# Outputs of the second layer's short row tiles transposed by DMA, their projection three slots later, expert weight pieces in the long row tiles

## What is computed

```python
q = (xn @ Wq).reshape(b, n, H, DH).transpose(0, 2, 1, 3) * scale
sim = jnp.einsum('bhid,bjd->bhij', q, k) + bias
sim = jnp.where(causal_mask, neg, sim)
sim = jnp.where(mask_p[:, None, None, :], sim, neg)
attn = jax.nn.softmax(sim, axis=-1)
out = jnp.einsum('bhij,bjd->bhid', attn, v)
out = out.transpose(0, 2, 1, 3).reshape(b, n, INNER)
out = out @ Wo
return layernorm(out, g_out)
```

## Time and profile before

| | |
|---|---|
| median of 3 runs | 1589.85 us (1588.85 to 1589.87) |
| the profiled execution, its own time | 1590.79 us |
| its span from first to last instruction | 1589.0 us |
| PE, DVE, ACT, POOL busy, share of the span | 89%, 85%, 70%, 57% |
| first layer, row tiles 0 to 7 | up to 692.6 us |
| second layer, short row tiles 8 to 11 | 692.6 to 917.9 us |
| second layer, long row tiles 12 to 15 | 917.9 to 1248.1 us |
| expert part | 1248.1 to 1589.0 us |

### The profile page before, as it was taken

One profiled execution on the slowest core, in us unless ns is written; L12 is line 12 of the kernel. 1 busy time (PEld: TensorE's weight loads), 2 busy tenths in 40 slices (PEclk: granted clock), 3 DMA queues, 4 the chain that ended last, 5 costly groups with the idle time before them and its releaser, 6 DMA issues. The chain is left out here.

```text
span 1589.0 us, 45236 instructions
## 1 busy us (share of the span) xinstructions
PE 1416.8 (89%) x15572; PEld 1063.1 (67%) x15572; DVE 1357.6 (85%) x3565; ACT 1117.0 (70%) x2933; POOL 902.1 (57%) x1766
## 2 busy tenths in 40 slices
PE   4777878888999999977789999999999899999998
PEld 2556656666777777765667777777778566666665
DVE  6667888999999999976788998989899888888887
ACT  4566778887989998866778888888888533333332
POOL 6766778775656556577776454535343466622222
PEclk9899999999999999999999999999999999999999
DMA  5001211122211232223333234444443100000000
GB/s 161 18 29 55 83 52 55 61 68 74 81 63 73 95 107 82 65 55 58 94 98 98 78 95 106 130 97 112 124 129 103 38 27 21 1 1 1 14 14 27
DMA packets 102177, 109.08 MB, mean 69 GB/s; under 512 B 55146, under 2 KB 78784, under 8 KB 101952
## 3 DMA queue, kind: packets, MB, share of 16 engines
q1 hardware_dynamic: 100644, 105.52, 23.4%
q10 hardware_dynamic: 1308, 0.67, 0.3%
HBM read 91.41 MB, written 2.17 MB: 59 GB/s over the span
## 5 line engine op out<-in xcount | busy, mean ns | idle before, releaser
L1431 DVE TENSOR_TENSOR p_lo<-tp,p_hi 128x256 f16<-128x256 f32 (+3 forms) x896 | 422.2, 495 | 94.6 <-ACT p_hi L1006 88.4
L1881 PE MATMUL tp<-ident,probs 128*128 128x128 f32 x2304 | 416.8, 281 | 14.4 <-DVE p_lo L1431 12.2
L1006 ACT ACTIVATE p_hi<-tp 128x256 f16<-128x256 f32 (+3 forms) x896 | 389.8, 445 | 46.6 <-PE tp L1881 28.5
L899 ACT ACTIVATE probs<-biased,neg_max 128x256 f32<-128x256 f32 (+7 forms) x512 | 395.5, 773 | 14.4 <-DVE neg_max L1327 12.1
L1741 PE MATMUL sc<-k_a,q_a 128*128 128x512 f16 (+3 forms) x768 | 254.1, 331 | 76.3 <-DVE neg_max L1327 59.3
L1525 PE MATMUL op<-v_s,p_hi 128*128 128x64 f16 x2304 | 297.2, 194 | 18.4 <-DVE o_raw L1303 9.2
L1881 PEld LDWEIGHTS tp<-ident,probs 128*128 128x128 f32 x2304 | 263.0, 141 | 57.1 <-DVE p_lo L1431 42.7
L1527 PE MATMUL op<-v_s,p_lo 128*128 128x64 f16 x2304 | 296.8, 193 | 0.0
L1526 PE MATMUL op<-v_s,p_hi 128*128 128x64 f16 x2304 | 296.8, 193 | 0.0
L1525 PEld LDWEIGHTS op<-v_s,p_hi 128*128 128x128 f16 x2304 | 219.8, 99 | 36.7 <-DVE o_raw L1303 21.0
L1742 PE MATMUL sc<-k_b,q_b 128*128 128x512 f16 (+3 forms) x768 | 241.4, 328 | 0.0
(11 more groups left out here) (359 smaller groups left out, 3479.3 us busy)
## 6 DMA issues: line engine op xcount, KB each, us to landing
bias<-rel_table SPq DMA_DIRECT2D x4, 2048.0 KB, 9.5
bias<-in_fside_16xSxS SPq DMA_DIRECT2D x4, 2048.0 KB, 9.0
bias<-rel_table SPq DMA_DIRECT2D x4, 1792.0 KB, 7.3
bias<-in_fside_16xSxS SPq DMA_DIRECT2D x4, 1792.0 KB, 8.8
bias<-rel_table SPq DMA_DIRECT2D x4, 1536.0 KB, 6.1
bias<-in_fside_16xSxS SPq DMA_DIRECT2D x4, 1536.0 KB, 7.6
bias<-rel_table SPq DMA_DIRECT2D x4, 1280.0 KB, 5.8
bias<-in_fside_16xSxS SPq DMA_DIRECT2D x4, 1280.0 KB, 6.8
```

What stands on the lines that cost most here:

```text
L899: ac.activation(probs[:, i % 2, 0:w], biased[:, i % 2, 0:w], ACT.Exp, bias=neg_max[:, u % 2, i % HU:i % HU + 1], scale=-1.0, accum_out=row ...
L1006: ac.activation(p_hi[:, gi % 4, 0:nb * P], tp[gi % 2][:, 0:nb * P], ACT.Copy)\
L1431: ve.tensor_tensor(p_lo[:, gi % 4, 0:nb * P], tp[gi % 2][:, 0:nb * P], p_hi[:, gi % 4, 0:nb * P], ALU.subtract).then_inc(s["p_lo"], 1)
L1881: last = te.transpose(tp[gi % 2][:, jj * P:(jj + 1) * P], probs[:, n % 2, (j0 + jj) * P:(j0 + jj + 1) * P], ident[:, :])
```

## The change

Three things. The outputs of units 64 to 95 are also cut in halves by POOL (halves_first) and transposed by SP's DMA (by_dma). Their projection, with its copy, its sum and the layer norm that follows, moves from slot 4(u + 2) to slot 4(u + 2) + 3 (y_slot), which is k = 3; there it goes through the bank aux. And the loads and pieces of jobs 6 to 9 move by 19 pairs of units: the pieces run from slots 384, 416, 448 and 480.

```diff
         def halves_first(u):
-            return u // UNITS % TILES >= TILES // 2
+            return u // UNITS % TILES >= TILES // 2 or by_dma(u)
...
         def by_dma(u):
-            return u // UNITS >= TILES + TILES // 2
+            return u // UNITS >= TILES
+
+        def late(u):
+            return TILES <= u // UNITS < TILES + TILES // 2
+
+        def y_slot(u):
+            return HU * (u + 2) + (HU - 1 if late(u) else 0)
...
         def load_at(jn):
-            return 4 * (jn - 3) + 1 + (TILES * HG // 2 if jn >= 6 else 0)
+            return 4 * (jn - 3) + 1 + (TILES * HG + 3 if jn >= 6 else 0)
```

Everywhere else the diff replaces the condition "k == 0" (and HU * (mu + 2) for the layer norm) by y_slot:

```diff
-                if k == 0 and 2 <= m <= NU + 1 and (m - 2) % UNITS >= B:
-                    u = m - 2
+                u = m - 2
+                if 2 <= m <= NU + 1 and u % UNITS >= B and n == y_slot(u):
                     pool.wait_ge(s["y_s"], u + 1)
...
-                    if n == HU * (mu + 2) + 1:
+                    if n == y_slot(mu) + 1:
                         pool.wait_ge(s["y_st"], p_ + 1)
...
-                if k == 0 and 0 <= m - 2 < NU:
-                    u = m - 2
+                u = m - 2
+                if 0 <= u < NU and n == y_slot(u):
                     layer, hg = u // U0, (u % UNITS) // B
                     take(False, (s["y_s"], u + 1))
```

More of the change, by code:

```diff
@@ L756, in _ @@
                         gp.tensor_tensor(y_rs[:, :], y_rs[:, :], mhalf[:, 0:1], ALU.pow).then_inc(s["y_rs"], 1)
-                    if n == HU * (mu + 2) + 3:
+                    if n == y_slot(mu) + 3:
                         pool.wait_ge(s["y_n"], p_ + 1)
@@ L1486, in _ @@
                         ve.bn_aggr(y_mv[:, :], y_st[:, :]).then_inc(s["y_st"], 1)
-                    if n == HU * (mu + 2) + 2:
+                    if n == y_slot(mu) + 2:
                         dve.wait_ge(s["y_rs"], p_ + 1)
```

## The result

The changed kernel takes 1602.5 us (median of 4 runs, 1601.3 to 1602.9) against 1589.9 of the kernel before beside it (1588.9 to 1590.1). The ratio is 1.0079, interval 1.0062 to 1.0097. The prediction was 1586.0 with a range to 1596: wrong in size and in sign.

The account below looks back on a forecast made before the run. It took POOL's list as the limit where slots are shortest, elsewhere a ring of PE, ACT and DVE. Terms: -10.9 + 0.5 + 4.5 + 1.1 + 1.0 = -3.8 us, giving 1586.0 us, range 1574 to 1596.

Parts of the forecast that it names:

- The bound: Row tiles 8 to 10: POOL's own list limits the shortest slots; tile 11: PE and DVE are nearly full.
- Tile 13: Row tile 13's start: job 7's load and piece make p_null 1.1 us late.
- ACT's waits for d_null: Row tiles 8 to 10: ACT's waits for POOL's d_null shrink from 7.4 to about 4 us.
- PE's wait for ot at the seam: Slot 392, between units 95 and 96: PE waits once for the transposed outputs, 0.5 us.
- The move of the projection: Row tiles 8 to 11: projecting three slots later, at k = 3, itself costs nothing.
- The gains of the slots: Row tiles 8 to 11 gain 4.0, 3.1, 2.0 and 1.8 us; in tile 11, 0.36 us per k = 2 slot.
- SP's queue: Row tile 9: bias rows and queries queue behind the outputs' transpose, 0.25 us for each of four pairs, 1.0 us.
- Tile 12: Row tile 12: 4.5 us waiting for the first weight piece, 0.5 at the seam, 1.0 for two overrunning units.
- B: Tiles 8 to 10: bias and queries late on SP's queue, 1.1 us a pair for 12 pairs; 1595 us, chance 0.17.
- C: Long tiles: POOL overflows with thirty 1.6 us pieces, 0.8 us in each of eight norm units; 1592 us, chance 0.13.
- A: Short tiles: whole ring relieved, DVE's 13.4 us return entirely and ACT's d_null waits vanish; 1576 us, chance 0.25.
- The clock: Row tile 8, granted clock 0.87: no effect counted, 2 us either way in the range.

Follow-up runs that it names:

- e4: Kernel before with only the loads and pieces of weight jobs 6 to 9 moved to the long row tiles: 1583.9 us (ratio 0.9962).
- e12: e4 with GpSimd's first piece of each moved job one unit later: 1583.5 us (ratio 0.9963).
- e15: e4 with the projection of tiles 8 to 11 three slots later and two ot buffers, transposes still on PE: 1584.5 us (ratio 0.9985).
- e11: e14 with the DMA transposes and late projection only from row tile 10 on: 1586.3 us (ratio 0.9982).
- e8: Changed kernel with the edits of both e6 and e7: 1589.8 us (ratio 1.0004).
- e6: Changed kernel with bias rows issued ahead of the outputs' transpose in tiles 8 to 11 only: 1595.3 us (ratio 1.0039).
- e7: Changed kernel with two buffers for the turned outputs (ot): 1591.7 us (ratio 1.0016).
- e13: Changed kernel with GpSimd's first piece of each of the five moved jobs one unit later: 1602.0 us (ratio 1.0085).
- e14: e8 with GpSimd's first piece of each moved job one unit later: 1588.0 us (ratio 0.9999).
- e5: Changed kernel with the loads back at their old pairs, leaving the DMA transposes and late projection alone: 1618.2 us (ratio 1.0178).
- e9: Changed kernel with the projection of tiles 8 to 11 back in its unit's first slot: 1610.0 us (ratio 1.0129).
- e16: Changed kernel with the second layer's bias rows, from tile 8's second pair on, issued on ScalarE's queue: 1606.8 us (ratio 1.0115).
- e10: e4 with outputs cut into halves on GpSimd in tiles 8 to 11 too, transposes still on PE: 1593.7 us (ratio 1.0026).
- e1: Changed kernel with the loads of weight jobs 6 to 9 issued three pairs of units earlier: 1604.4 us (ratio 1.0091).
- e18: e12 with the second layer's bias rows issued on ScalarE's queue: 1590.6 us (ratio 1.0010).

## Why the prediction was wrong, by its own steps

**What was right.** The bound was read rightly where the expert pieces are concerned: in tiles 8 to 10 GpSimd's list sets the pace, and with the pieces out ACT no longer waits for d_null. Tile 8 got 5.6 us shorter in e4 at a clock of 1.00 and 4.0 in e12 at 0.93, where the whole change had been given 4.0. Tile 13 came at +1.1 us, the predicted 1.1. ACT's waits for d_null fell from 7.4 us to 1.9, where 4 was predicted. PE's wait for ot at the seam is there, 1.09 us against 0.5, and only one more of 0.6 besides, so the three slots were enough. PE's timeline at the seam:

```profile
947.05 0.27 PE L1533 MATMUL aux<-wo,ot 128*128 128x256 f16 x1 [1.09 <-DMA ot<-o]
```

The move of the projection cost little in sum, as predicted (e15: nothing to some 4 us), but it was not nothing slot by slot, as the next point shows.

**The gains of the slots.** ACT's timeline in row tile 11, two exponentials with a k = 2 slot between them:

```profile
885.33 0.71 ACT L907 ACTIVATE probs<-biased,neg_max 128x512 f32<-128x512 f32 x1
...
886.81 0.71 ACT L907 ACTIVATE probs<-biased,neg_max 128x512 f32<-128x512 f32 x1
```

The slot takes 1.48 us against 1.89 in the earlier trace rows: the predicted 0.36 and a little more. But a shorter slot is not a shorter tile. Tile 11 gained 1.0 of 1.8, and without the queue's trouble tiles 10 and 11 of e11 gained 1.6 and 1.3 against e4 (predicted 2.0 and 1.8). That looks like the right mechanism at three quarters of its size. e15 says otherwise: it keeps the transposes on PE and has 0.9 and 1.2 of the same gain, from the move of the projection alone. What the removed transposes add, less what comes in their place, is 0.1 us in tile 11, and in tile 10 between -0.1 (e8) and 0.8 (e11). So this term of the sum came near its size by luck, by a part of the change that the prediction had put at nothing.

**The step that failed: SP's queue.** The prediction had the whole mechanism in sight: bias rows behind an outputs' transpose that waits for a later projection, queries behind the bias rows, 9.5 to 11.4 us of chain for 8.1 + 0.7 of slots. By that sum the price is 0.7 to 2.6 us a pair. The prediction took 0.25, less than its own short end, and in tile 9 alone: 1.0 us. Measured: 23.0 us of GpSimd's waits in 16 pairs, 1.4 us a pair on average, 7.0 of them in tile 9 and 12.8 in tiles 10 and 11, for which nothing was counted. Not all of a wait is lost: e8, which leaves 0.6 us of them, has tiles 8 to 11 7.4 us shorter. The bias rows of the quoted pair took 5.3 us, the short end of what was assumed; it was the sum of SP's waits ahead of them that was too small. SP stands for the late projection 29 times in the 32 units. e6 and e7, each taking one link out of that chain, give back 7.2 and 10.8 us, together 12.7: 7.4 in tiles 8 to 11 and 5.1 in tile 12. "Taken near the short end, since POOL is late there anyway" was the choice that lost: GpSimd was late because of the weight piece, which the same change removes.

**Tile 12.** Predicted 4.5 + 0.5 + 1.0 us, measured 8.8. The piece's wait was there and longer than 4.5 (ACT stands 6.2 us): the bias rows went out 3.2 us after the tile's first exponential, where the prediction had 2.5, and the weights landed at 14.8, where it had 13.4. But that wait wasn't the whole cause. e13 took it away and the tile lost 1.1 us. The queries' transpose lands behind the same load, and the prediction, which gave that behaviour with its rows, applied it to bias rows only. PE's own waits for q_b there are 5.4 us. About 2.8 us of the miss are here, 12.4 in tiles 8 to 11: together 15.2, the difference of the span from the predicted one. Of the 12.4, SP's queue accounts for 7.4 (e8); the other 5.0 are mostly tile 9, 51.9 us in e8 where 48.9 was predicted, and stay open (below).

**The rivals.** B, SP's queue takes over, was the case that came: its 1.1 us a pair lie between the 1.4 that GpSimd waited and the 0.5 that were lost by it (7.4 in 16 pairs). It was priced without the queries behind the weights in tile 12 and without what tile 9 lost besides, hence 1595 and not 1602. Its own sum is unclear: it takes "about 3 more lost" off the 12 instead of adding it. C, GpSimd overflows in the long tiles, didn't occur: tile 14 +0.4, tile 15 nothing. A fell with B.

**The clock.** The granted clock of tile 8 is 0.84, before 0.87; in e4 it is 1.00. What a lower clock costs can be read where the change touches nothing. Busy time of row tile 1 (columns as above) of before and then of e4, the same code:

```profile
107.77:174.67 66.90, 52.63 (x556) 42.25 (x556) 52.44 (x177) 49.10 (x168) 46.90 (x102) 1.00 0.19 55
```
```profile
107.72:178.19 70.47, 56.51 (x556) 45.00 (x556) 52.55 (x177) 49.30 (x169) 47.02 (x102) 0.93 0.17 52
```

The profiled execution of e4, the longest of its eight (1587.9 us), loses 3.6 us there, and that of the kernel before doesn't. In tile 8 the same: e12 has it as e4 has it, at 0.93 and 47.4 us instead of 1.00 and 45.8. So some 1.6 us of tile 8, and perhaps more, are not the edit's. Busy time of row tile 8 of e8, without PE's transposes, and of e15, with them:

```profile
692.16:740.46 48.30, 32.89 (x363) 25.99 (x362) 30.25 (x138) 29.22 (x128) 35.57 (x73) 0.89 0.32 62
```
```profile
691.86:741.37 49.51, 36.71 (x381) 28.84 (x381) 32.79 (x144) 30.88 (x135) 29.50 (x61) 0.86 0.25 46
```

By the rule of the Trainium skill, TensorE: Matmul & The Clock Gate, section Part 4: PE-mode transpose, transposes don't count; these two rows don't speak against it. But one pair doesn't settle it. Over all runs tile 8 lies at 0.77 to 0.90 where its outputs are transposed by DMA, and at 0.86 to 1.00 where PE transposes and the weight pieces are gone. In tile 9, e4, e12 and e15 have 1.00, e8 and e14 0.93. The lowest, 0.77 to 0.79, are those of e5, e9 and e16, whose tile 8 is also the longest (55.7 to 58.9 us): the clock is low where PE waits most. Whether the missing transposes lower it besides, no run separates.

**What stays open.** e14 is still 4.1 us above e4 (5.9 by the ratios). Its rows put 2.5 in tile 8 and 2.0 in tile 9, of both of which the clock may hold a part or all (0.89 and 0.93 against 1.00 and 1.00), 1.9 in tile 12 (the queries behind the weights), less 2.0 in tiles 10 and 11. Whether the rest of tiles 8 and 9 is GpSimd's halves wasn't isolated, since e10 made PE wait for them instead. The best kernel measured is e12, or e4 within the scatter: 1583.5 us, 0.4% below the kernel before, without any transpose moved.

## What to carry to other kernels

Split a change of two parts before judging it: here one line was worth -6 us and the rest +18.6, or +29.6 without that line. Where a queue waits for a consumer's release before it issues one small transfer, everything behind it inherits that wait; a second buffer for that transfer gave back 10.8 us, the better order 7.2, and each helped in another place. And a small transfer that someone waits for must not be issued while a bulk load is under way or about to be: moving the load in time moves the cost (e1), letting its reader come later changes only the name of the wait (e13), and moving it to another queue does not remove it (e16, e18). Last, when an edit moves one step and removes another, run each alone: the gain booked for the removed transposes was the moved projection's (e15).

## What the runs showed of the hardware

A DMA transpose of the outputs (128 x 512, 2 bytes) holds the issuing queue for 1.19 us and lands 2.4 us after its issue when nothing else is under way. With a 512 KB load beside it, it takes longer: the queries' transpose, 0.67 us behind the load on the same queue, 5.8 us, 1.2 after the load's landing; the outputs', 0.27 us ahead of the load on another queue, 5.8 us, 0.3 after it. With 1.25 MB of bias rows and 1 MB of weights ahead of it, the queries' transpose took 10.5 us, as the landings of the issues from 922.5 to 925 us show (the weights' KB are misprinted there, as in the earlier trace rows):

```profile
stage<-in_L_cond_w_gate SPq DMA_DIRECT2D x1, 0.5 KB, 10.8
q_a<-q_n SPq DMA_TRANSPOSE x1, 10.5
```

I had not expected that a load issued after a transpose, on another queue, delays it.
